# A decoder layer on one core: when the experts' answers come back, and another order of one turn of self-attention

## The reference

```
x = x + self_attention(layernorm(x))           # 16 heads of 64, causal, then @ w_o
x = x + cross_attention(layernorm(x), ctx)     # 16 heads of 16, relu on q, k, v
x = x + ffn(layernorm(x))
ffn(X): X = X + small_attention(rmsnorm(X))    # 4 heads over one shared key and value
        xf = rmsnorm(X); rw = softmax(xf @ Wr.T + bias); take the best 2 of 8 experts
        out = X + shared_expert(xf) + sum over the 2: weight * expert(xf)
expert(t) = (silu(t @ w1.T) * (t @ w3.T)) @ w2.T
```

## Time and profile before

| | us |
|---|---|
| median of three runs | 2072.44 |
| the profiled execution's own time | 2051.32 |
| span of its instructions | 2049.4 |
| PE busy | 1841.0 (90%) |
| DVE busy | 1427.5 (70%) |
| ACT busy | 1292.7 (63%) |
| POOL busy | 1097.4 (54%) |

### The profile page before, as it was taken

One profiled execution on the slowest core, in us unless ns is written; L12 is line 12 of the kernel. 1 busy time (PEld: TensorE's weight loads), 2 busy tenths in 40 slices (PEclk: granted clock), 3 DMA queues, 4 the chain that ended last, 5 costly groups with the idle time before them and its releaser, 6 DMA issues. The chain is left out here.

```text
span 2049.4 us, 40880 instructions
## 1 busy us (share of the span) xinstructions
PE 1841.0 (90%) x13992; PEld 973.4 (47%) x13992; DVE 1427.5 (70%) x3320; ACT 1292.7 (63%) x2477; POOL 1097.4 (54%) x1102
## 2 busy tenths in 40 slices
PE   4799999999999999879999999986999999689984
PEld 2456666666666666542333323322333344356653
DVE  5566666666666666547787777775688888756666
ACT  2677676767676776636777777782666666435542
POOL 2466666666656665633344323322667776646554
PEclk9899999999999999978999999997999999889996
DMA  6322222223222232233322133201001110224356
GB/s 181 77 63 63 63 63 63 64 62 67 70 63 63 64 72 63 63 58 63 63 55 38 35 63 63 53 16 37 22 21 45 48 49 27 86 75 127 104 174 208
DMA packets 102395, 141.00 MB, mean 69 GB/s; under 512 B 16272, under 2 KB 66224, under 8 KB 102192
## 3 DMA queue, kind: packets, MB, share of 16 engines
q1 hardware_dynamic: 95280, 119.44, 24.9%
q0 software_dynamic: 6912, 18.95, 2.6%
HBM read 53.77 MB, written 33.90 MB: 43 GB/s over the span
## 5 line engine op out<-in xcount | busy, mean ns | idle before, releaser
L771 POOL TENSOR_TENSOR a_P_lo<-a_PR,a_P_hi 128x384 f16<-128x384 f32 (+1 forms) x384 | 377.7, 998 | 335.8 <-ACT a_P_hi L580 227.9
L1333 DVE TENSOR_REDUCE x_NM<-x_pm 128x1 f32<-128x512 f32 x512 | 342.1, 687 | 98.9 <-PE x_pm L1069 96.5
L1254 ACT ACTIVATE x_PR<-x_pS 128x512 f32<-128x512 f32 x512 | 300.8, 601 | 111.9 <-PE x_pS L1085 105.7
L700 DVE CUSTOM_DVE_ANT_0 a_pm<-a_pm,a_causal 128x128 f32<-128x128 f32 (+3 forms) x512 | 249.3, 505 | 153.9 <-PE a_pm L463 146.5
L577 ACT ACTIVATE a_PR<-a_pS 128x384 f32<-128x384 f32 (+1 forms) x384 | 201.9, 526 | 123.5 <-PE a_pS L486 115.4
L580 ACT ACTIVATE a_P_hi<-a_pS 128x384 f16<-128x384 f32 (+1 forms) x384 | 201.4, 524 | 6.5 <-PE a_pa L500 5.7
L1097 PE MATMUL x_pa<-x_PR,x_V 128*32 128x256 f32 x2048 | 167.7, 400 | 1.7
L484 PE MATMUL a_pS<-a_QA,a_KA 128*128 128x512 f16 (+3 forms) x512 | 152.7, 301 | 12.2 <-DMA a_QB<-a_NMT 5.4
L463 PE MATMUL a_pm<-a_KA,a_QA 128*128 128x128 f16 (+3 forms) x512 | 139.4, 303 | 23.1 <-DVE a_NM L700 11.3
L500 PE MATMUL a_pa<-a_P_hi,a_V_hi 128*128 128x512 f16 (+3 forms) x512 | 152.1, 300 | 2.2 <-DVE a_Y L710 1.3
L500 PE MATMUL a_pa<-a_P_hi,a_V_lo 128*128 128x512 f16 (+3 forms) x512 | 153.8, 300 | 0.0
(11 more groups left out here) (411 smaller groups left out, 5033.3 us busy)
## 6 DMA issues: line engine op xcount, KB each, us to landing
a_QA<-a_nat_q_hi SPq DMA_DIRECT2D x128, 128.0 KB, 2.3
first_keys<-sent SPq DMA_DIRECT2D x80, 129.0 KB, 2.5
a_QB<-a_nat_q_lo SPq DMA_DIRECT2D x64, 128.0 KB, 2.4
a_KA<-a_nat_k_hi SPq DMA_DIRECT2D x64, 128.0 KB, 2.3
a_KA<-a_nat_k_lo SPq DMA_DIRECT2D x64, 128.0 KB, 2.4
a_KB<-a_nat_k_hi SPq DMA_DIRECT2D x64, 128.0 KB, 2.4
e_ga<-back SPq DMA_DIRECT2D x16, 512.0 KB, 6.2
first_keys<-in_w SPq DMA_DIRECT2D x12, 512.0 KB, 3.7
```

The lines of the kernel that those rows point to most:

```text
L700: eng.tensor_tensor_reduce(out=pm[i % 2][:, 0:n], in0=pm[i % 2][:, 0:n], in1=causal[:, T - n:T], scale=1.0, scalar=NEG, op0=ALU.add, op1=A ...
L771: eng.tensor_tensor(P16[1][:, m % RH, 0:n], PR[:, m % RF, 0:n], P16[0][:, m % RH, 0:n], ALU.subtract).then_inc(s_el, 1)
L1254: eng.activation(PR[:, kc, j, :], pS[i % 2][:, :], ACT.Exp, scale=SCALE).then_inc(s_e, 1)
L1333: eng.tensor_reduce(NM[:, v % 2, c:c + 1], ring_bank("max", v, n)[:, :], AX.X, ALU.max, negate=True).then_inc(s_red, 1)
```

## The change

Two parts that touch different stages.

1. Self-attention: all times in `PLACE` are replaced; TURN and the threads outside it stay. On POOL and for the copies on SP the order within the units stays the same. On PE the order within one turn (from QK 0 of u; M is MX; -1 and -2 the earlier units) changes

2. Experts:

```diff
-    GB, EB, IB = 2, 3, 6
+    GB, EB, IB = groups[0].count, 3, 6            # 6 buffers ga
 def tensor_program:
-        for p in range(NP + 2):
-            if p < NP:
-                hidden(p)
-            if 1 <= p <= NP:
+        for p in range(NP):
+            hidden(p)
+            if p >= 1:
                 turn_hidden(p - 1)
             if p + 1 < NP:
                 turn_rows(p + 1)
             if p >= 2:
                 make(p - 2)
+        make(NP - 2)
+        turn_hidden(NP - 1)
+        make(NP - 1)
 def gpsimd_program:
-        for p in range(NP + 3):
+        for p in range(NP + 2):
             if p < NP:
                 low(p)
             if p < TT:
                 scatter(p)
-            if p >= 3:
-                send_back(p - 3)
+            if p >= 2:
+                send_back(p - 2)
 def come_back(b):
+                after(eng, s_ga[b % 2 * 2 + h], 16 * (b // 2))
 def store_out(b, h):                              # half a batch, 256 KB, as soon as it is combined
 def sync_program:
             rows.load(eng, p)
-            if p == FIRST_BACK:
-                for b in range(GB):
-                    come_back(b)
+            if 0 <= p - FIRST_BACK < groups[0].count:
+                come_back(p - FIRST_BACK)
 ...
+        for b in range(groups[1].first):           # after all loads
+            for h in range(2):
+                store_out(b, h)
+        for b in range(groups[1].first, B):
+            come_back(b)
+        for b in range(groups[1].first, B):
+            for h in range(2):
+                store_out(b, h)
```

More of the change, by code:

```diff
@@ L295, in self_attention @@
     PLACE = {
[L296 to L318, removed]
@@ L319, in self_attention @@
-        ("SP", "CKB"): (19.676,),
-        ("SP", "NP"): (44.562,),
+        ("PE", "QK"): (0, 5.124, 10.378, 12.651),
+        ("PE", "V"): (18.782, 19.596),
+        ("PE", "WO"): (24.638, 25.068),
+        ("PE", "MX"): (19.627, 19.631, 21.566, 22.294, 24.709, 24.88, 25.098, 26.111, 29.915, 31.477, 31.97, 32.546, 34.927, 36.966, 38.051, 39.257),
+        ("PE", "NM"): (41.181,),
+        ("PE", "S"): (45.1, 45.819, 47.374, 48.229, 50.954, 51.851, 55.954, 57.623, 63.622, 66.216, 69.22, 69.536),
@@ new lines, in self_attention @@
+        ("PE", "AV"): (48.99, 52.53, 53.693, 58.584, 61.396, 61.4, 69.509, 70.385, 71.292, 72.007, 72.016, 72.528),
+        ("ACT", "QK"): (0.587, 5.128, 13.255, 15.71),
+        ("ACT", "V"): (21.662, 24.661),
+        ("ACT", "NM"): (42.17,),
+        ("ACT", "E"): (45.108, 45.82, 49.07, 51.668, 51.676, 52.454, 56.974, 58.374, 66.448, 68.025, 70.575, 70.579),
+        ("ACT", "H"): (45.611, 48.227, 49.847, 51.671, 52.274, 53.126, 58.358, 63.826, 66.961, 68.035, 70.578, 70.585),
+        ("ACT", "LN"): (56.797, 64.894, 71.3, 72.562),
@@ new lines, in self_attention @@
+        ("ACT", "EX"): (66.825, 72.566),
+        ("DVE", "QK"): (5.916, 8.692, 13.259, 18.344),
+        ("DVE", "V"): (22.981, 24.665),
+        ("DVE", "WO"): (25.075,),
+        ("DVE", "MX"): (19.85, 20.856, 24.22, 24.226, 24.872, 24.881, 26.456, 26.664, 31.482, 31.487, 34.926, 34.936, 36.784, 39.256, 39.258, 39.639),
+        ("DVE", "Y"): (66.836, 71.486, 73.763, 73.774),
+        ("POOL", "LO"): (46.404, 48.455, 51.828, 53.705, 58.365, 58.366, 60.686, 63.827, 66.962, 68.036, 70.706, 71.307),
@@ L321, in self_attention @@
+        ("POOL", "SP"): (73.194, 74.256),
+        ("SP", "CQ"): (15.561,),
+        ("SP", "CK"): (19.104,),
+        ("SP", "CKB"): (33.758,),
+        ("SP", "NP"): (45.09,),
     }
@@ L2604, in moe_experts @@
     s_st = [sem(f"stored{n}") for n in range(EB)]
-    s_ga, s_cmb, s_out = [sem(f"came_back{n}") for n in range(2 * GB)], sem("combined"), sem("out")
+    s_ga, s_cmb, s_out = [sem(f"came_back{n}") for n in range(4)], sem("combined"), sem("out")
     pairs, firsts = rows.pairs, rows.firsts
@@ L2746, in combine @@
             b, t, n = returns[i]
-            eng.wait_ge(s_ga[b % GB * 2 + t // HT], 16 * (b // GB + 1))
+            eng.wait_ge(s_ga[b % 2 * 2 + t // HT], 16 * (b // 2 + 1))
             if n == 1:
@@ L2829, in come_back, with store_out @@
             for h in range(2):
+                after(eng, s_ga[b % 2 * 2 + h], 16 * (b // 2))
                 eng.dma_start(ga[:, b % GB, h * HT:(h + 1) * HT, :, :],
                               back[2 * T * b + h * T:2 * T * b + (h + 1) * T, :].rearrange("(t p n) c -> p t n c", p=P, n=2))\
[L2832 to L2836, removed]
+                   .then_inc(s_ga[b % 2 * 2 + h], 16)
+        def store_out(b, h):
+            ts = slice(b * TT + h * HT, b * TT + (h + 1) * HT)
+            eng.wait_ge(s_cmb, 2 * TT * b + TT * (h + 1))
+            eng.dma_start(out_dram[:, ts, :], x_res[:, ts, :]).then_inc(s_out, 16)
         for p in range(XB, NP):
@@ L2848, in sync_program @@
                 rows.tail(eng, 1, p - TAILS)
[L2849 to L2860, removed]
+        for b in range(groups[1].first):
[6 more added lines that the diff above has]
+                store_out(b, h)
+        eng.wait_ge(s_out, 32 * B)
     with nc.Block() as block:
```

## The result

The changed kernel took 2057.68 us (median of 11 runs, 2046.12 to 2062.36). The kernel before, run beside it, took 2073.08. The ratio of the comparable runs is 0.9931, 95% interval 0.9912 to 0.9949, so 14.3 us less (10.5 to 18.2). Forecast: 7.4 less, 2065, range 2047 to 2079.

The account below looks back on a forecast made before the run. PE was taken as the bound in self-attention, busy 667.7 of 689 us. Experts -9.7 and self-attention +2.3 sum to -7.4, so the median 2072.4 becomes 2065, range 2047 to 2079.

Parts of the forecast that it names:

- The stall: Experts: DVE's 7.80 us wait for batch 2's transfer goes whole with six buffers; -7.8, bounds 7.0 to 8.0.
- the 8 that I had named as a sign of being wrong: Experts: prediction is wrong if they end less than 8 us sooner after their beginning.
- Answers a pair sooner: Experts: POOL's earlier sending costs nothing in steady pairs but delays early pairs with two scatters; +1.0 (0 to 1.3).
- The end: Experts: six transfers instead of eight after the last low part, -2.4; last store half as large, -0.5.
- The start: Self-attention's first turns: SP issues the maxima about 1.5 earlier in the third turn, 1 before; -2.5 (-5 to +2).
- rival 2: Self-attention: the new turn has no gaps and the start gains 5; -20 in all, 2052; chance 0.20.
- Ordinary turns: Self-attention: turns without a new batch meet every wait and stay at 24.46; 0 (0 to +7).
- The turn before a batch: Self-attention: new idle 3.05 against 2.7, including 1.9 before AV 9; +0.4, seven times: +3 (-10 to +8).
- The turns with the next stage's weights: Self-attention: DVE's weight split ahead of M 8 gives 1.5 idle instead of 0.6 in two turns; +1.8 (0 to 3).
- the clock falls: Self-attention: the gap before AV 9 brings half clock, costing 12 over seven turns; +4.6 in all, 2077; chance 0.12.
- ordinary turns miss: Self-attention: Y 0 behind M 15 comes 0.3 to 0.7 late in 24 turns; +7 to +17, 2072 to 2082; chance 0.12.
- the experts' gain given back: Experts: early batches share the DMA with loads and DVE waits elsewhere; about 3 of 9.7 stay, 2072; chance 0.08.

Follow-up runs that it names:

- y0: The unchanged kernel before, profiled a second time; 2048.0 us.
- z0: The changed kernel run again beside the kernel before, on another chip; 2025.95 us, ratio 0.9913.
- x1: The kernel before with only the new order of self-attention's turn; ratio 0.9963 to the kernel before, 7.7 us less.
- x2: The kernel before with only the new experts, old order of the turn; ratio 0.9955 to the kernel before, 9.3 us less.
- y1: The changed kernel with PE turning the next pair's rows ahead of the previous pair's hidden layer; ratio 0.9882 to the kernel before.
- y2: The changed kernel with POOL's second transfer of a pair waiting for the turned rows; ratio 0.9879 to the kernel before.
- z1: y1 repeated, now beside the changed kernel; 2020.45 us, ratio 0.9899 to the kernel before.
- z2: y2 repeated, now beside the changed kernel; ratio 0.9915 to the kernel before, within 0.1 us of the changed kernel.
- w2: The kernel before with three weight chunks of the start split sooner on ACT and DVE; ratio 0.9982 to the kernel before, 3.7 us less.
- x4: The kernel before with only POOL's answers sent a pair sooner; ratio 0.9989 to the kernel before, 2.3 us less.

## Why the prediction was right, and where it was off

The measured time, 2057.7, is in the range and 7 under the forecast; at 0.7% less it is past the 0.5% that I had given 0.36. Two sums stand behind the forecast. The one for the experts was right. The one for self-attention had the wrong sign. That the total is inside the range is the work of the range's width, 15 us below the forecast: the forecast's own 2059 to 2070 it misses by 1.

**Experts, -9.7 forecast, -9.3 measured, and -9.9 in the traces of the 5.11 kind** (from the first low part to the end, 238.5 in y0 and 228.6 in z0). At the slow pace it is less, -7.9 (258.3 in x1, 250.2 in after and 250.6 in x2), because less of the stall is left to win; that is just under the 8 that I had named as a sign of being wrong.
- The stall, -7.8: right. y0 shows it again, and z0 has its six combines in each pair with nothing waited for and 5.68 a pair, as forecast (DVE in y0, then in z0; they answer to the earlier trace rows):

```profile
1993.41 0.88 DVE L2751 SCALAR_TENSOR_TENSOR x_res<-e_ga,m_weight,x_res 128x256 f32<-128x256 f32 x2 [7.54 <-DMA e_ga<-back]
```

```profile
1977.26 2.45 DVE L2753 SCALAR_TENSOR_TENSOR x_res<-e_ga,m_weight,x_res 128x256 f32<-128x256 f32 x6
...
1982.94 2.45 DVE L2753 SCALAR_TENSOR_TENSOR x_res<-e_ga,m_weight,x_res 128x256 f32<-128x256 f32 x6
```

  At 5.77 a pair only about 6 are left of it: x1's stalled step is 12.2, not 13.6.
- Answers a pair sooner, +1.0: right. The first seven steps of the low parts take 35.67 in y0 and 36.72 in z0, and 40.35 in x1 and 41.22 in after.
- The end, -2.4 and -0.5: measured -2.6 and -0.7 (the 0.7 with the reordered products in it). The sixth transfer starts 6.80 after the last low part ends (2045.03 - 2038.23), forecast about 7, and the last answer, copied 2.2 after DVE's copy, is there in time.

**Self-attention, +2.3 forecast, -5.4 in the traces** (first score of cross-attention at 919.3 on average over five traces of the old turn, 913.8 over seven of the new, y1, y2, z1 and z2 among them; the runs say -7.7, 2.9 to 12). The step that failed is the start.
- The start, -2.5: measured -6.0 (89.9 to 83.9 on average). The order and the 1.5 that SP gains were read rightly. I priced them at their length and left the clock out, although two half-clock stretches, near 80 and 100 us, stand at such waits in before. The traces split by that: in after, where two such stretches remain, the gain is only 1.6; in the five traces of the new order that have none it is 7.2 (89.9 to 82.7). My rival 2 had it at 5.
- Ordinary turns, 0: right, 24.46.
- The turn before a batch, +0.4 each: measured 0.0 in the pair of turns shown and -0.4 on average over the six pairs behind the start (52.9 to 52.5 in the same twelve traces), and the account of it was wrong. I took the normalised x at 2.9 from the earlier trace rows, where POOL works on low parts beside it; in the new order POOL has a gap there, x takes 1.4, and AV 9 waits 0.2 instead of 1.9. In exchange M 15 waits 1.0 instead of 0.55 and M 0 0.5 instead of none.
- The turns with the next stage's weights, +1.8: after 53.07 for the two, before 50.87, so +2.2. Two later turns that the sum did not name are longer, 26.38 instead of 24.46 and 28.4 instead of 27.2 on average, and one is 1.6 shorter. From the fourth to the 32nd maxima the new order is 2.1 longer (718.9 against 716.8 on average), where the terms gave 4.6 (7 x 0.4 + 1.8). The 0.4 was itself rounded up: 3.05 - 2.7 is 0.35.
- Behind the last turn 1.3 us go (65.9 to 64.6), which the sum didn't have.

The Trainium skill, "SBUF — State Buffer", section "SBUF: two separate sides", states that VectorE and GpSimd share one pair of ports and that the loser waits out the other's whole instruction. The section names conditions for it, such as a mode in which VectorE uses both of its port pairs; no run here shows which mode these instructions were in. The rows agree with the rule. One normalisation of the earlier trace rows and the low part beside it:

```profile
619.97 0.96 POOL L771 TENSOR_TENSOR a_P_lo<-a_PR,a_P_hi 128x384 f16<-128x384 f32 x1
620.09 1.00 DVE L647 TENSOR_SCALAR a_xn<-x_res,a_mv,a_rstd 128x256 f32<-128x256 f32 x1
```

The normalisation starts 0.12 after the low part starts and ends 0.16 after it ends. In the seven turns of before that stand ahead of a batch the four normalisations take 0.43, 1.00, 1.00 and 0.69, and all 28 end 0.15 or 0.16 behind the end of an instruction of POOL. Beside an idle POOL one takes 0.40.

**The rivals.** 1, the clock falls: not seen, half clock in self-attention behind the start stands only near 796 us, for 3.4, as before; the wait it hung on was 0.2. 2, no gaps: half of it came, the start's 5, while the turns behind gained nothing in sum. Its price was added up wrongly, too: its terms give 21 to 24, not 20. 3, ordinary turns miss: no, 24.46. 4, the experts' gain given back: no, except for some 2 at the slower pace.

What stays open: why the signal of the turned rows is late on some chips. It follows the chip, not the kernel, and keeps time with POOL's transfers, but no run here removed it there. How the 6 us of the start divide between wait and clock is an estimate; only w2 tried one part of it alone. The stretch of cross-attention varies by up to 20 us (461 to 481 between its first and last scores in x1 to x4) with no edit to it, so a single trace's span can't carry a difference of 10.

## What to carry to other kernels

Before adding a forecast to a median, check that the profiled execution has the pace of the timed runs: the one used here was 1% under the median and turned out to be a different baseline, not noise. Where rows show half clock at a wait, price that wait at both clocks. Take a duration for a moved instruction from a place where the same neighbours work beside it, not from its old place.

## What the runs showed of the hardware

- One handover in the experts' loop differs between chips: ACT starts 0.04 us behind the last of eight transposes, or 0.50 to 1.00 behind it and then always 1.5 to 1.6 behind the start of one of POOL's indirect transfers. Over 38 pairs that is about 25 us. Another handover from PE to ACT in the same loop is 0.04 in both.
- A DVE normalisation of 128x256 f32 took 0.40 us alone. In a train beside POOL's subtractions one got through per instruction of POOL, 1.00 us each in the middle of the train.
- Two copies of 2 KB issued right behind a 512 KB load were used 3.4 to 4.0 us after their issue in eleven traces and 4.8 and 5.0 in two; ahead of it, within 3.3 in the one trace tried.
- In the third turn of the start, idle times of 1.3 to 1.9 us left the clock at full (six traces), and with 3.1 to 4.4 it was at half near 80 us (seven traces). Length alone does not decide: near 790 us an idle of 1.94 was followed by half clock in two of six traces of the old turn, one of 2.1 in six of eight of the new, and in w2 an idle of 2.88 near 98 us was not. In y0 and x4 idles of 2.16 and 2.29 near 525 us were, where 1.44 in before was not. The Trainium skill, "TensorE: Matmul & The Clock Gate", section "Part 1: The HAM clock gate", states that an idle TensorE falls back to half rate; the rows agree, and the shorter idles were free of it in some traces and not in others.
